# A fused attention and FFN layer on one core: query items stored as whole tiles, a rebuilt start, and two kinds of DMA issued by GpSimd instead of SyncE

## The reference

```python
def bitnet_linear(x, weight, scale_param):
    s = jnp.maximum(jnp.mean(jnp.abs(weight), axis=1), 1e-08)
    y = jnp.einsum('bsi,oi->bso', x, jnp.sign(weight / s[:, None]))
    return jnp.nan_to_num(y * (s * scale_param)[None, None, :], nan=0.0, posinf=1e6, neginf=-1e6)

def binary_diff(w, base):                       # W1, W2, W3 of the FFN
    d = w - base
    return base + jnp.mean(jnp.abs(d)) * jnp.sign(d)

x = x + attention(layernorm(x))                 # 32 heads of 16, 8 key/value heads, q, k, v and output by bitnet_linear
x = x + (silu(h @ W1.T) * (h @ W3.T)) @ W2.T    # h = layernorm(x), inner width 1792
```

## Time and profile before

| | |
|---|---|
| runs of the kernel before | 999.89, 1002.71, 1000.87 us; median 1000.87 |
| profiled execution | 1002.98 us, its span 1001.2 us |
| PE busy | 949.4 us, 95% |
| DVE busy | 712.7 us, 71% |
| ACT busy | 553.4 us, 55% |
| POOL busy | 299.2 us, 30% |
| mean granted TensorE clock | 0.975 |

### The profile page before, as it was taken

How to read it: one execution, slowest core, us unless ns; L and a number is a source line. 1 busy time by engine, 2 the same in 40 slices (tenths; PEclk the granted TensorE clock), 3 DMA queues, 4 the chain that set the end, 5 groups by cost and what they waited for, 6 DMA issues and landing times.

```text
span 1001.2 us, 14700 instructions
## 1 busy us (share of the span) xinstructions
PE 949.4 (95%) x4962; PEld 615.3 (61%) x4962; DVE 712.7 (71%) x950; ACT 553.4 (55%) x1078; POOL 299.2 (30%) x306
## 2 busy tenths in 40 slices
PE   6599999999999999988899999999999999999997
PEld 5344443444344433333578888888888888888886
DVE  5677898789877889867965588655886558854443
ACT  5448888998999989965853322423223232232220
POOL 4735658356636531535011101011110111101110
PEclk9669999999999999998999999999999999999999
DMA  5724667576646676623840002310023100220001
GB/s 191 192 75 138 188 192 192 159 215 168 196 133 188 172 219 211 186 87 97 261 164 33 1 1 84 117 57 0 0 84 122 51 0 0 84 85 0 0 0 42
DMA packets 77701, 109.74 MB, mean 110 GB/s; under 512 B 6737, under 2 KB 30289, under 8 KB 77649
## 3 DMA queue, kind: packets, MB, share of 16 engines
q1 hardware_dynamic: 76912, 108.23, 36.1%
q10 hardware_dynamic: 416, 0.66, 0.2%
q0 software_dynamic: 320, 0.20, 0.1%
HBM read 75.17 MB, written 32.77 MB: 108 GB/s over the span
## 4 chain that ended last, share of the span: by engine, by line
PE 80%; DVE 6%; ACT 4%; DMA 3%; issue 2%; POOL 2%; SPq 2%; DVEq 0%; POOLq 0%; ACTq 0%
PE psum L1613 15%; PE psum L1614 15%; PE psum L1615 15%; PE psum L1514 9%; PE psum L1504 8%; PE psum L1488 6%; DVE nmx L1158 3%; PE psum L1417 3%; PE psum L1603 2%; ACT probs L987 2%; DMA k_slot<-k_stack 2%; PE psum L1418 2%; PE psum L1525 2%; PE psum L1526 2%; DMA q_stack<-q_lo 1%
## 5 line engine op out<-in xcount | busy, mean ns | idle before, releaser
L1158 DVE TENSOR_REDUCE nmx<-psum 128x2 f32<-128x1024 f32 x256 | 305.0, 1221 | 63.8 <-PE psum L1488 61.6
L987 ACT ACTIVATE probs<-psum 128x512 f32<-128x512 f32 x512 | 271.3, 602 | 44.1 <-PE psum L1504 42.6
L847 POOL CAST dh<-w2T 128x512 fp32r<-128x512 f32 (+1 forms) x56 | 50.9, 909 | 423.4 <-PE psum L1615 392.0
L1613 PE MATMUL psum<-fxh,wh 128*128 128x512 f32 x448 | 174.6, 390 | 2.2 <-DVE wl L1340 2.2
L1614 PE MATMUL psum<-fxl,wh 128*128 128x512 f32 x448 | 174.5, 389 | 0.0
L1615 PE MATMUL psum<-fxh,wl 128*128 128x512 f32 x448 | 174.3, 389 | 0.0
L1504 PE MATMUL psum<-q_slot,k_slot 50*128 50x512 f32 x512 | 149.0, 473 | 13.1 <-ACT probs L987 7.6
L1504 PEld LDWEIGHTS psum<-q_slot,k_slot 50*128 50x128 f32 x512 | 64.1, 187 | 128.1 <-ACT probs L987 60.0
L1514 PE MATMUL psum<-probs,v_slot 128*32 128x512 f32 x1024 | 138.7, 614 | 0.0
L1347 DVE TENSOR_TENSOR gate<-gate,psum 128x512 f32<-128x512 f32 x56 | 38.4, 686 | 132.2 <-PE psum L1615 129.9
L1045 ACT ACTIVATE hh<-gate 128x512 fp32r<-128x512 f32 x56 | 35.4, 632 | 162.0 <-DVE gate L1347 162.0
(11 more groups left out here) (133 smaller groups left out, 1318.2 us busy)
## 6 DMA issues: line engine op xcount, KB each, us to landing
stage<-in_L_ffn_mean_w_dram SPq DMA_DIRECT2D x84, 256.0 KB, 4.6
q_slot<-q_stack SPq DMA_DIRECT2D x62, 192.0 KB, 3.5
stage<-in_L_ffn_w_dram SPq DMA_DIRECT2D x42, 256.0 KB, 5.5
q_stack<-q_hi SPq DMA_DIRECT2D x32, 256.0 KB
weighted_values<-u_sb SPq DMA_DIRECT2D x32, 256.0 KB, 3.9
k_slot<-k_stack SPq DMA_DIRECT2D x62, 96.0 KB, 3.7
q_stack<-q_lo SPq DMA_DIRECT2D x16, 256.0 KB
an<-weighted_values SPq DMA_DIRECT2D x16, 256.0 KB
```

The lines of the kernel that those rows point to most:

```text
L847: nc.gpsimd.tensor_copy(dh[parity][:], w2T[:, bass.ds(src, 1), :].rearrange("p o c -> p (o c)")).then_inc(dh_ok, 1)
L987: nc.scalar.activation(probs[kt][:, j, :], BANK[ring_bank(("score", g, kt, j))], ACT.Exp, scale=HEAD_DIM ** -0.5).then_inc(exp_ok, 1)
L1158: v.tensor_reduce(column, pair, AX.X, ALU.max, negate=True).then_inc(s_max, 1)
L1613: mm(o, lhs_hi, rhs_hi, start=first, stop=False)
```

## The change

The text of the diff has four parts.

1. **Layout of the queries.** The rows of the query weights are loaded in another order, 16 DMAs of 32 rows instead of two, so that a whole `q_hi` tile can be stored as it lies, once. `q_stack` holds it once, and the loads of a group read the high part twice. A query item has two stores where it had three; the keys still have three. `load_group` is 8 DMAs instead of 4, for the same bytes.
2. **The start.** Group 1 too is filled from SBUF. Item QT+1 comes ahead of the values, three items instead of two and a fourth are projected before the first scores, the others in pieces between score steps. `WARM` is 64 instead of 40.
3. **Item stores** are issued by POOL right behind `split_item`.
4. **Loads of FFN weights** (`load_difference`) are issued by POOL, in the slices with kt = 1. Those of the last five loads of the mean weights (lines 603 to 611) stay on SP.

```diff
-ITEMS = (KTILE, QT, VTILE, QT + 1, QT + 2, QT + 3)
+ITEMS = (KTILE, QT, QT + 1, VTILE, QT + 2, QT + 3)
-VT_AT = 16
-STORE_AT = (8, 12, 16, 20, 24)
-SELECT_AT = (6, 11)
+VT_AT = 19
+SELECT_AT = (0, 4, 8)
+ITEM_PIECES = {2: (4, 0), 3: (4, 1), 10: (5, 0), 11: (5, 1)}
-    q_dram = nc.dram_tensor("q_stack", [GROUPS, REP, ROWS, SEQ], ...)
+    q_dram = nc.dram_tensor("q_stack", [BATCH, 4, 2, P, SEQ], ...)
-    WARM = 40
+    WARM = 64
...
     def load_group(eng, g, s, done):
+        b, m, pair = g // KV_HEADS, g % KV_HEADS // 2, g % 2
         for h in range(2):
-            eng.dma_start(q_slot[s][HALF * h:HALF * h + ROWS].bitcast(FP32),
-                          q_dram[g, 2 * h:2 * h + 2].rearrange("j r t -> r j t")).then_inc(done, 16)
+            heads = slice(HALF * pair + 32 * h, HALF * pair + 32 * (h + 1))
+            for part in range(3):
+                r = HALF * h + HEAD_DIM * part
+                eng.dma_start(q_slot[s][r:r + HEAD_DIM].bitcast(FP32),
+                              q_dram[b, m, (0, 0, 1)[part], heads, :].rearrange("(d j) t -> d j t", j=2)).then_inc(done, 16)
             eng.dma_start(k_slot[s][HALF * h:HALF * h + ROWS].bitcast(FP32), k_dram[g]).then_inc(done, 16)
...
-        sp.dma_start(w_nat[:, QT, :], q_w[0:P, :]).then_inc(w_in[1], 16)
-        sp.dma_start(w_nat[:, QT + 1:QT + 4, :], ...).then_inc(w_in[2], 16)
+        for t in range(KT):
+            for h in range(4):
+                rows = slice(t * P + 32 * h, t * P + 32 * (h + 1))
+                sp.dma_start(w_nat[32 * h:32 * (h + 1), QT + t, :], q_w[rows, :].rearrange("(j d) c -> d j c", j=2)
+                             ).then_inc(w_in[1 if t == 0 else 2], 16)
...
@@ gpsimd: store_item, called behind split_item
+        def store_item(b, i):
+            c = 5 * b + i
...
+                rows = q_dram[b, ITEMS[STORED[i]] - QT]
+                pool.wait_ge(qh_ok, c + 1)
+                nc.gpsimd.dma_start(rows[0], hi).then_inc(part_out[c % Q_RING], 16)
+                pool.wait_ge(ql_ok, c + 1)
+                nc.gpsimd.dma_start(rows[1], lo).then_inc(part_out[c % Q_RING], 16)
...
@@ gpsimd: pool_slice
                     if now == ITEM_AT[i] + PRED_LAG and i != VALUES:
                         split_item(b + 1, i)
+                        store_item(b + 1, STORED.index(i))
...
+            if kt == 1 and g % 2 == 1 and g // 2 + 1 < IT:
+                load_difference(g // 2 + 1, 0)
+            if kt == 1 and g % 2 == 0 and 0 < g // 2 < IT:
+                load_difference(g // 2, 1)
...
@@ tensor: the start
-        for m in (KTILE, VTILE, QT):
+        for m in (KTILE, VTILE):
             transpose_signs(m)
         for t in range(TT):
+            if t == 2:
+                transpose_signs(QT)
             pe.wait_ge(xn_ok, t + 1)
...
         first_item(1)
+        transpose_signs(QT + 1)
+        pe.wait_ge(signs_ok, 4)
         first_item(2)
-        for m in (QT + 1, QT + 2, QT + 3):
-            transpose_signs(m)
+        transpose_signs(QT + 2)
+        transpose_signs(QT + 3)
+        first_item(3)
+        pe.wait_ge(signs_ok, OT)
```

More of the change, by code:

```diff
@@ L674, in _, with load_scale @@
         pool.wait_ge(const_ok, 5)
-        for src, t0, tiles in ((k_s, KTILE, 1), (q_s, QT, 4), (v_s, VTILE, 1), (o_s, OT, 4)):
-            nc.gpsimd.dma_start(scl[:, t0:t0 + tiles], src.rearrange("(t p) -> p t", p=P),
-                                allow_slow_non_contiguous=True).then_inc(scl_in, 16)
+        def load_scale(dst, src, done):
+            nc.gpsimd.dma_start(dst, src, allow_slow_non_contiguous=True).then_inc(done, 16)
+        load_scale(scl[:, KTILE:KTILE + 1], k_s.rearrange("(t p) -> p t", p=P), scl_in)
+        for j in range(2):
+            load_scale(scl[j:P:2, QT:QT + 1], query_scale(0, j), scl_in)
+        load_scale(scl[:, VTILE:VTILE + 1], v_s.rearrange("(t p) -> p t", p=P), scl_in)
         def token_factor(b):
@@ L757, in _, with load_pair, load_difference @@
         fill_values(1)
+        norm_tokens(1, 2)
         norm_tokens(1, 3)
-        guard_item(0, 4)
-        split_item(0, 4)
+        store_item(0, 3)
         guard_item(0, 5)
+        def load_pair(e, dst, sources):
+            for k in range(2):
+                nc.gpsimd.dma_start(dst[:, k, :], sources[k][bass.ds(e * P, P), :]).then_inc(fw_in[e % 3], 16)
+            nc.gpsimd.dma_start(dst[:, 2, :].rearrange("p (t c) -> p t c", c=P),
+                                sources[2][:, bass.ds(e * P, P)].rearrange("(t p) c -> p t c", p=P)).then_inc(fw_in[e % 3], 16)
+        def load_difference(e, part):
+            if part == 0:
+                if e >= 3:
+                    pool.wait_ge(facc_ok, 3 * (e - 2))
+                    pool.wait_ge(fsgn_ok, 3 * (e - 2))
+                load_pair(e, wn[e % 3], (w1, w3, w2))
+            else:
+                if e >= 2:
+                    pool.wait_ge(fd_ok, 3 * (e - 1))
+                load_pair(e, mn[e % 2], (m1, m3, m2))
         def difference(e, k):
@@ L907, in _ @@
             magnitude(m)
-        act.wait_ge(w_in[1], 16)
+        act.wait_ge(w_in[1], 64)
         magnitude(QT)
@@ L945, in _ @@
             sign_tile(m)
-        scale_item(0, 4, 4)
         for m in range(OT, WTILES):
@@ L1407, in transpose_tokens, with project_item @@
             last.then_inc(xT_ok, 1)
-        def project_item(b, i, bank, half=None, first=False):
+        def project_item(b, i, bank, half=None, first=False, pieces=(0, KT)):
             m = ITEMS[i]
@@ L1413, in project_item @@
             c = slice(0, SEQ) if half is None else slice(HSEQ * half, HSEQ * (half + 1))
-            for kt in range(KT):
+            for kt in range(*pieces):
                 if first:
```

206 lines of the change are left out of this document (98 added, 108 removed).

## The result

The changed kernel is slower: 1037.91 us median (1029.66 to 1043.66, 6 runs) against 1001.16 (998.06 to 1002.72, 6 runs), a ratio of 1.0338 with a 95% interval of 1.0301 to 1.0375 (the quotient of the two medians is 1.0367). The forecast was 996.9, and the time lies far above the range of 990 to 1007. The profiled execution has a span of 1027.9 us (1001.2 before).

The account below looks back on a forecast made before the run. PE was taken to bound the whole span, so only the start and attention could change: 1002.98 - 7.0 - 1 + 4 = 999.0 us for the profiled execution, 996.9 as a median, range 990 to 1007.

Parts of the forecast that it names:

- SyncE's side: Attention, SP's queue: less ahead of its group loads, longer load_group covered by lead; -1 us (0 to -1.6, or +1).
- GpSimd's side, +4: Attention, ends of batches 0 and 1: POOL's added DMA issues delay subtractions and then PE; +4 us (0 to 7.7).
- the priced path: End of batch 0: seven POOL issues delay the third subtraction, then ACT's sign instruction, exponentials and PE; 4.0 us.
- Rival A: Batch ends: POOL becomes the bound at 1.15 us an issue, +13.4 in place of +4, 1006.3 us; chance 0.22.
- Locking out by VectorE: POOL's DMA issues: the skill says DVE can lock GpSimd out of writing descriptors; not seen in the trace, no size.
- The start, -7: From the beginning to the first shifted score: slot 1's wait gone, item 3 moved ahead; -7.0 us (-2 to -13).
- the 52 to 56 named: Sign that the forecast is right: the first shifted score of slice 0 comes at 52 to 56 us.
- C: Start: gains only 2 us, PE at half clock or slots filled no earlier; 1001.9 us; chance 0.20.
- B: Start and first slices: the clock stays up, gaining 11 in place of 7; 992.9 us; chance 0.22.
- chance of 0.22 for slower: Whole kernel: the chance given to a time slower than 1003.9 us.

Follow-up runs that it names:

- group load first: Changed kernel with SyncE issuing the group load ahead of the shift's copy, GpSimd still issuing FFN loads and stores: 1019.32 us, ratio 1.0159.
- both on SyncE: Changed kernel with FFN loads and item stores both issued by SyncE again: 1000.92 us, ratio 0.9972; repeated on another chip 1001.66 us, 1.0004.
- bytes cut: Changed kernel with GpSimd's FFN loads of tiles 3 to 13 cut to an eighth of their columns: 1019.29 us, ratio 1.0189.
- slice 3: Changed kernel with GpSimd's FFN loads issued at slice 3 of a group instead of slice 1: 1024.23 us, ratio 1.0227.

## Why the prediction was wrong

**The step that failed** is the one on SyncE's side: "`load_group` is four issues longer, at 0.48 us about 2 us of SP in a group, covered by the three groups of lead", in a term booked at -1. There are no three groups. A slot for group g+3 is asked for in group g, but the scores run ahead by 14 steps (`n = 8 * g + 2 * kt + S_AHEAD`), so it is first read in slice 1 of group g+1, and SyncE comes to the load only after the shift of group g+1. The trace shows 9.6 us from the shift's copy to the need, for eight issues and a landing. That was in sight: 1.6 us of the waits of the earlier trace rows lay in attention, so the load of before already arrived just in time now and then. The term was not -1 but about +18 (changed kernel 1.0338, with the group load first 1.0159).

What made the load late was not its eight pieces by themselves, but what GpSimd's queue moves beside it, on a lead that the pieces had made shorter. The prediction weighed what GpSimd's issues cost GpSimd, and took the traffic to be gone from SyncE's way ("less ahead of them"). In the kernel before the FFN pieces stood behind the group load in one queue, and I take the order of the queue to have worked as a priority; that the issuer decides is shown, how the transfers share the DMA engines is not seen directly. What happens between two queues the Trainium skill says on its page "DMA: Bandwidth & Descriptors" (section "Issuing engines are not separate DMA queues"): DMAs started by different engines run on the same 16 DMA engines and interleave. The trace agrees (landing of `k_slot` 3.3 us median and 7.2 at most, against 2.4 and 4.4 with one issuer), and I had weighed other rules of that page and not this one.

**GpSimd's side, +4.** The price was right: 0.55 to 0.57 us for a plain piece, 0.76 for the w2 piece, 0.55 to 0.66 for the stores, 78 us for the 126 issues against "about 75". (GpSimd's busy row does count its own issues, other than I wrote of all engines' rows: 381.1 us, against 304.5 with both on SyncE.) The line of the FFN pieces:

```profile
L774 POOL DMA_DIRECT2D stage<-in_L_ffn_w_dram x28: 537/552/641, 58.7 to 397.9; - x28
L775 POOL DMA_DIRECT2D stage<-in_L_ffn_w_dram x14: 754/762/772, 59.9 to 398.4; - x14
```

The place was right as well, the end of batch 0 with its seven issues. The path was not: ScalarE was to wait about 4 us for a subtraction there and waited 1.9 in two waits (none near 250 us, as forecast), and TensorE's first hole came through the mask, VectorE's selection and its maxima, which the forecast left out. The two kinds of issue can be told apart. With the stores alone on GpSimd TensorE waits 2.41 us for the maxima, and the clock is 0.62 at 150 to 160 us; with the FFN loads alone it waits 1.27 for them and then 2.48 for the exponentials, the priced path, and the clock is 0.86. The term was also mis-sized: memsets of 58 us in all the former places cost 7 to 10 us, and after the slots were given their lead 16 were still lost. I had priced the wait once, at full clock. TensorE pays it again at the lower clock level, as the windows at 150 to 170 us show. How the 16 divide between this, the stores' traffic and smaller waits is not settled. Rival A named the wait of VectorE for a guard, at 1 us, and had the right engine, but the wrong condition: it was to decide from 0.87 us an issue, and the issue cost 0.57; its 1.15 us stand in no row. Locking out by VectorE was not to be seen: the longest plain FFN issue took 0.66 us.

**The start, -7.** The first score was to come at 30.5 us, and came at 30.91 (the earlier trace rows has 30.92); the first shifted score was to come 23.3 us later and came 25.1 later, at 56.06 (the earlier trace rows has 60.86):

```profile
30.91 0.73 PE L1535 MATMUL psum<-k_slot,q_slot 48*128 48x512 f32 x4 [1.52 <-DMA q_slot<-q_lo]
...
56.06 0.50 PE L1551 MATMUL psum<-q_slot,k_slot 50*128 50x512 f32 x2 [0.94 <-ACT fac_row L986]
```

So 4.8 of 7.0, within its bounds; 56.06 is at the very edge of the 52 to 56 named. It is the fastest execution, though: three other kernels with the same start have the first shifted score at 57.56 (bytes cut), 59.00 (slice 3) and 59.35 (group load first), gains of 3.3 to 1.5, and the last two lie beyond the 58 that I had named as the sign of C. The wait for slot 1, is gone, and the clock at 12 to 14 us is up (1.00), but it is 0.62 and 0.50 in the windows at 30 to 50 us. What the sum had left out is the same thing as above, on a smaller scale: 2 MB of tokens and o_w stand in SyncE's queue ahead of the first slots' copies, as in the kernel before. With o_w behind them the first shifted score came at 55.05 in a kernel that has the stores on SyncE, and at 59.09 and 57.73 in the two runs of that kernel without it. So the kernel with both on SyncE gained only 1.8 to 3.1 us in the start, not the 4.8 that I had in mind in its later expectations, and this is part of why it was only level.

**Rivals.** B (the clock stays up) did not happen: the clock fell at 30 to 50 us as before, and then more often. C (the start gains 2) did not happen in the profiled execution and came near in others, and would not have made the kernel slower. Of the chance of 0.22 for slower 0.19 went to one mechanism, GpSimd's time, and none by name to late slots.

The loss of 3.4 points of ratio, put together: late slots 1.8; GpSimd's time 0.7 to 1.0 or more; less the gain of the start, 0.2 to 0.5. One point or so is left over, for what the parts do to each other.

## What to carry to other kernels

Before moving DMAs off a busy queue ask what their place in it protected: behind the urgent load in one queue they wait for it, in a queue of their own they run against it, and a small urgent copy behind large ones (6.7 us here) is the same question turned round. Count the lead of a load from the first instruction that reads it, in code that runs ahead, and from the point at which its issuer comes to it. Ask also whom the delayed engine serves first: here a mask for VectorE came ahead of the subtraction for ScalarE that I had priced. And price a hole of the bounding engine above its length where the clock is seen to fall behind such holes. How far above stays open: late slots were worth 11.6 us between two profiled executions, about as much as the idle time that went, and about 18 between the medians.

## What the runs showed of the hardware that was not expected

SyncE's own issues become slower at busy moments: three pieces of 64 KB took 3.68 us in the changed kernel, against 1.26 to 1.35 in quiet groups. The traffic need not come from another engine: with both on SyncE three took up to 2.55, and a single issue up to 1.7. The software queue itself was no slower in landing: an FFN piece of 256 KB landed 3.8 to 4.3 us after GpSimd issued it, and 3.8 after SyncE did with both on SyncE. What costs, as I read it, is that it lands beside, not behind.

The granted clock fell behind short holes. In the changed kernel TensorE stood 2.36 us until 148.46, and the clock is 1.00 until 148 and 0.50 from 149 us on; with the memsets it stood 2.06 us until 145.03, and the clock is 0.50 from 147 us on. Behind the 1.27 us of the kernel before, at the same place, it stayed at 1.00.
